# A transformer layer with routed experts on one core: residual sums and their statistics moved ahead of the routing in VectorE's step

## What is computed

```python
# attention: Q, K, V are products of the normed x with wq, wk, wv (64 x 256 each)
energy  = einsum('bnd,bne->bde', K, V)
context = einsum('bnd,bde->bne', Q, energy) * sqrt(3/64)
x = x + einsum('bnd,ed->bne', context, wo)

# experts, on xn = layernorm(x)
scores = sigmoid(xn @ Wr)                       # 8 scores per token
_, idx = top_k(scores + router_bias, 2)
w  = take_along_axis(scores, idx); w = w / (sum(w) + 1e-9)
cw = zeros((T, 8)).at[rows, idx].add(w)
hid = silu(xn @ Wg[e]) * (xn @ Wu[e])           # e = 0..3, 256 -> 128
routed = sum_e cw[:, e] * (hid @ Wd[e])
routed += (cw[:, 4] + cw[:, 6]) * xn + cw[:, 7] * relu(xn)
shared = causal depthwise convolution of xn with 4 taps + conv_b
x = x + routed + shared
```

## Time and profile before

| | |
|---|---|
| median of 3 runs | 970.82 us (967.7 to 972.82) |
| the profiled execution: time, span | 970.19 us, 968.4 us |
| PE matmul busy | 917.5 us, 95% of the span |
| PE weight loads busy | 808.8 us, 84% |
| VectorE busy | 814.6 us, 84% |
| GpSimd busy | 553.8 us, 57% |
| ScalarE busy | 506.0 us, 52% |
| mean granted clock of TensorE | 0.983 |
| chain that ended last, by engine | PE 55%, DVE 26%, ACT 6%, POOL 6%, issue 5% |

### The profile page before, as it was taken

How to read it: one execution, slowest core, us unless ns; L and a number is a source line. 1 busy time by engine, 2 the same in 40 slices (tenths; PEclk the granted TensorE clock), 3 DMA queues, 4 the chain that set the end, 5 groups by cost and what they waited for, 6 DMA issues and landing times.

```text
span 968.4 us, 16869 instructions
## 1 busy us (share of the span) xinstructions
PE 917.5 (95%) x5816; PEld 808.8 (84%) x5816; DVE 814.6 (84%) x2294; ACT 506.0 (52%) x1003; POOL 553.8 (57%) x491
## 2 busy tenths in 40 slices
PE   4779999999999999999999999999999999988887
PEld 4668989888898888998898988988898988777776
DVE  6667889999889988999888998899888987776685
ACT  3454655555465555556555654656565545534432
POOL 2135755556576555656655566666556655655653
PEclk9788999999999999999999999999999999999989
DMA  6311333222133332223333211333322122221111
GB/s 178 116 44 45 109 110 110 99 99 77 56 110 110 110 109 71 72 78 110 110 109 110 89 68 65 110 110 110 110 88 80 41 79 88 88 88 66 65 64 47
DMA packets 61014, 87.10 MB, mean 90 GB/s; under 512 B 4480, under 2 KB 56832, under 8 KB 56832
## 3 DMA queue, kind: packets, MB, share of 16 engines
q1 hardware_dynamic: 60928, 86.01, 25.9%
HBM read 68.96 MB, written 17.04 MB: 89 GB/s over the span
## 4 chain that ended last, share of the span: by engine, by line
PE 55%; DVE 26%; ACT 6%; POOL 6%; issue 5%; DMA 1%; POOLq 0%; ACTq 0%; DVEq 0%
PE ps_gu L359 7%; PE ps_gu L361 7%; PE ps_gu L360 7%; PE ps_sh L464 5%; PE ps_y L359 4%; PE ps_y L360 4%; PE ps_y L361 4%; ACT x L676 4%; DVE stats L820 3%; POOL rstd L1012 3%; DVE acc L812 3%; PE ps_sh L454 2%; DVE chosen L863 2%; PE ps_y L407 2%; DVE hid L774 2%
## 5 line engine op out<-in xcount | busy, mean ns | idle before, releaser
L1030 POOL TENSOR_TENSOR gate<-gate,cwb 128x512 f32<-128x512 f32 x128 | 174.4, 1363 | 191.4 <-ACT gate L617 115.6
L359 PE MATMUL ps_gu<-x2T_hi,wgu_hi 128*128 128x512 f32 x512 | 212.7, 415 | 0.8 <-DVE hid L774 0.8
L360 PE MATMUL ps_gu<-x2T_lo,wgu_hi 128*128 128x512 f32 x512 | 203.3, 397 | 0.0
L361 PE MATMUL ps_gu<-x2T_hi,wgu_lo 128*128 128x512 f32 x512 | 203.1, 397 | 0.0
L1047 POOL TENSOR_TENSOR enx<-inv_e,logits 128x32 f32<-128x32 f32 x32 | 177.1, 5533 | 7.2 <-ACT logits L610 7.0
L617 ACT ACTIVATE gate<-ps_gu 128x512 f32<-128x512 f32 x128 | 76.0, 594 | 160.6 <-PE ps_gu L361 160.6
L359 PE MATMUL ps_y<-wd_hi,hid_hi 128*128 128x256 f32 x512 | 153.0, 299 | 4.0 <-POOL hid_lo L1035 3.5
L361 PE MATMUL ps_y<-wd_hi,hid_lo 128*128 128x256 f32 x512 | 145.1, 283 | 0.0
L360 PE MATMUL ps_y<-wd_lo,hid_hi 128*128 128x256 f32 x512 | 145.1, 283 | 0.0
L791 DVE SCALAR_TENSOR_TENSOR conv<-x2T,conv_w,conv 128x512 f32<-128x512 f32 x192 | 141.0, 773 | 0.0
L1009 POOL TENSOR_TENSOR mv<-mv,eps_ln 128x4 f32<-128x4 f32 x64 | 12.8, 199 | 184.1 <-DVE mv L823 156.5
(11 more groups left out here) (94 smaller groups left out, 1961.0 us busy)
## 6 DMA issues: line engine op xcount, KB each, us to landing
cwb<-cw_rows SPq DMA_DIRECT2D x32, 1024.0 KB, 4.7
xa<-in_x SPq DMA_DIRECT2D x32, 512.0 KB, 6.9
acc<-in_x SPq DMA_DIRECT2D x32, 512.0 KB, 5.9
out<-acc SPq DMA_DIRECT2D x64, 256.0 KB, 2.3
cwb<-in_wg SPq DMA_DIRECT2D x4, 128.0 KB, 2.7
cwb<-in_wu SPq DMA_DIRECT2D x4, 128.0 KB, 2.6
cwb<-in_wd SPq DMA_DIRECT2D x1, 512.0 KB, 4.1
cw_rows<-cwT SPq DMA_DIRECT2D x32, 8.0 KB, 1.3
```

The source lines that it names most:

```text
L359: nc.tensor.matmul(dst, a_hi, b_hi, start=start, stop=False, skip_group_check=True)
L360: nc.tensor.matmul(dst, a_hi, b_lo, start=False, stop=False, skip_group_check=True)
L361: return nc.tensor.matmul(dst, a_lo, b_hi, start=False, stop=stop, skip_group_check=True)
L1030: g.tensor_tensor(gate[:, e % 2], gate[:, e % 2], cwb[:, q, e], ALU.mult).then_inc(gatew_ready, 1)
```

## The change

Only VectorE's order inside a step changes; no instruction is added or removed. The first residual sum now stands in front of the third expert's product, the second one and the statistics directly behind it, and the routing after them. The third expert's low half follows the routing, then the fourth expert's product, then the relu term. Steps in which the routing works and the experts don't keep their order.

```diff
--- before.py
+++ after.py
@@ -954,24 +954,23 @@
                     dve.wait_ge(mhi_out, st.chains(1, 1))
                     v.tensor_tensor(m_lo[:, :, :], ps_gram[:, :].rearrange("p (c n) -> p c n", c=HC),
                                     m_hi[:, :, :].bitcast(F32), ALU.subtract).then_inc(mlo_out, 1)
+                if b_on:
+                    residual(st, 0)
+                if c_on:
+                    hidden(st, 2)
+                if b_on:
+                    residual(st, 1)
+                    norm2_stats(st)
+                if r_on:
+                    route(st)
+                if c_on:
+                    hid_low(st, 2)
+                    hidden(st, 3)
                 if c_on:
 
                     dve.wait_ge(relu_ready, st.before("C", TG, TG))
                     k = st.slot("C", 4)
                     v.tensor_tensor(acc[:, k], acc[:, k], x2[:, st.slot("C", 2)], ALU.add).then_inc(relu_added, 1)
-                    hidden(st, 2)
-                if r_on and c_on:
-                    route(st)
-                if c_on:
-                    hid_low(st, 2)
-                if b_on:
-                    residual(st, 0)
-                    residual(st, 1)
-                    norm2_stats(st)
-                if r_on and not c_on:
-                    route(st)
-                if c_on:
-                    hidden(st, 3)
                 if st.on("A"):
                     for c in range(HC):
                         q = st.slot("A", 4)
```

## The result

The changed kernel took 990.56 us (median of 4 executions, 983.2 to 993.5), the kernel before 970.04 us beside it: a ratio of 1.0196, 95% interval 1.0149 to 1.0243. In a later comparison it took 991.2 against 971.4 us, 1.018 (1.0142 to 1.0218). A ratio here is estimated with its interval and is not the quotient of the two medians beside it, which can lie some 0.4% off (here it is 1.021). The profiled execution is the quickest of its four, 983.2 us with a span of 981.4.

A forecast was written before the change was run, and what follows sets the result against it. TensorE was taken to bound most of the run. Late routing +21.1, the L454 wait -5.8 and the tail -1.8 gave +13.5 on 970.19, 983.7 us, stated as 984.0 for a median; 8-in-10 range 972 to 991.

The forecast's parts named there:

- TensorE is the bound, and two waits decide: At full load TensorE runs matmuls 112.07 of 112.43 us; VectorE's order matters only through what TensorE waits for.
- The wait before L454 goes: At x2_transpose 0, 100 to 829 us: earlier statistics remove TensorE's wait for the normed tiles x2, -5.8 us.
- The routing comes late by the hold: GpSimd's gate_weight 3 holds den 0.75 us; TensorE loses 0.81 us up to expert 2's down product, 26 steps: +21.1 us.
- No further cost behind the down product: After expert 2's down product, hidden 3 and the relu term end before ScalarE can begin x2; cover 0.7 us.
- The tail: From 827 us, without the Gram matrix: three steps 0.91 us shorter each, the first 0.9 longer, sum -1.8 us.
- The last two steps: The last two steps, without attention, gain or lose a few tenths of a microsecond.
- The sum: Whole kernel: +21.1 - 5.8 - 1.8 = +13.5 us on the profiled 970.19, giving 983.7; 984.0 us for a median.
- No hold: At den beside gate_weight 3: den and what follows get through while GpSimd works; 961 us, chance 0.08.
- part of the hold: In the routing: den slips through, the next two-tensor instruction is held only 0.3 us; 970 us, chance 0.13.
- more hold: gate_weight 3 slips and holds routing up to 1.3 us, or the relu term is held; 989 to 994 us, chance 0.10.
- rival 4: The same as more hold: 0.2 to 0.4 us more in a step, 989 to 994 us, chance 0.10.
- Slack on TensorE: TensorE's weight loads leave 12.89 of 112.43 us free, absorbing the wait for routing; 962.6 us, chance 0.04.

The follow-up runs named there:

- The first experiment: The changed kernel with one more wait on GpSimd, so gate_weight 3 starts only after the routing's third instruction: 966.1 us, ratio 0.9904 to the kernel before.

## Why the prediction was right, point by point

- **TensorE is the bound, and two waits decide.** Right. VectorE and GpSimd lost 35 and 24 us of busy time and nothing was gained by it.
- **The wait before L454 goes (-5.8).** Right; none is left. ScalarE's order was what came next.
- **The routing comes late by the hold (+0.81 a step, +21.1).** Right in each figure: den 0.89 us (reckoned from zero + 2.72 to + 3.61, 0.89), L499 at zero + 7.33 (7.33), the down product at zero + 8.13 (8.12). The first experiment takes the hold away and with it the loss. Four steps grew by 2.25 us; 4 x 0.81 less three waits of 0.34 before L454 is 2.2. Over the whole body, 25 steps, the profiles differ by 14.7 us; the 21.1 less 5.8 of the prediction, for 26 steps, are 15.3.
- **No further cost behind the down product.** Right for the new order. The relu term's cover held: it ends at 558.54 and x2 starts at 559.53. For the old order I carried the same reasoning over and was wrong, since I had looked at who waits for the relu term and not at whom it holds.
- **The tail (-1.8).** Right as a count of work, wrong as a forecast of time, because the clock is missing from it. TensorE is through x2_transpose 0 at zero + 12.8 wherever the clock is full (12.86 reckoned), and the four tail steps of the kernel with 12 idle products take 112.9 us against 114.9 before, -2.0. In the changed kernel itself they take 115.5 us in the first profile and 119.4 in the second: +0.7 and +4.5.
- **The last two steps (a few tenths).** This term was mis-sized. From the end of these four steps to the end of the span the kernel before takes 49.85 us and the changed one 46.6 in both profiles, -3.2. The granted clock there is 0.91 to 0.92 in the kernel before and 1.00 in the changed one. How much of the 3.2 us the clock makes was not separated.
- **The sum (983.7).** It met the profiled execution (983.2) partly by luck: the +0.7 instead of -1.8 in the tail steps and the -3.2 at the end cancel. A slip of 0.3 us stands in the last line too: 13.5 over the median of 970.82 is 984.3, not 984.0. The median is 990.6, 6.6 us above the forecast and 0.4 us inside the range, whose upper end had been drawn for more hold and not for the clock; that it lies inside is luck. The sum was put against one execution and took over its granted clock, while the kernel before runs at 0.982 in the median and the changed one at 0.973 to 0.974.
- **The rivals.** No hold, part of the hold and more hold are refuted by den's 0.89 us in the median of 32 and by the transposes at zero + 7.33. By the time alone the measured 990.6 us would have been rival 4's (989 to 994). Slack on TensorE by its weight loads is refuted as well: with weight loads running for 99.88 of 111.70 us the fastest of these steps had no idle time between matmuls, and each wait of the changed kernel appeared in the step's length. The Trainium skill (Trainium Kernel Development and Optimization, section Best Practices) would have seen room there; these rows show none.

## What to carry to other kernels

Before moving a chain of small VectorE instructions, lay GpSimd's instructions beside the new place as well as the old: an instruction of 0.14 us became one of 0.89 because a 1.29 us product began 0.44 us before it, and moving that product by one semaphore was worth 1.3% in the kernel before, while the reordering cost 2%. Ask of a moved instruction both what holds it and what it holds. And reckon idle time of TensorE twice, once as time and once as clock: filling waits of 2.9 us in the tail brought back some 6 to 7 us of granted clock. A sum made against one profile carries that profile's clock with it, on both sides of the comparison.

## What the runs showed of the hardware

- VectorE and GpSimd hold each other in both directions. den, chosen and raw (128x32 elements in SBUF), and wsum_eps (128x4, up to 0.96 us), when they start inside a GpSimd product, end 0.03 to 0.06 us behind it. The relu term, begun 0.07 us earlier, stretched GpSimd's power from 1.01 to 2.00 us. Batch norm aggregates (four in 0.36 us), maxima (four in 0.35 us) and sums with one operand in PSUM (0.67 to 0.69 us) passed beside the same product at their usual length. The Trainium skill (GPSIMD Engine Reference, section Key points) names the contention, with VectorE instructions that read two SBUF inputs or run in a 2-port mode. The rows of the two-input instructions agree and show its size here: the whole rest of the other's product. GpSimd's power is different: in the changed kernel one runs from 539.74 for 5.43 us, and VectorE's hid_lo, with two inputs, starts inside it at 541.34 and takes its usual 0.68. Whether den, which reads one tile, runs in such a mode no row shows.
- Twelve useless products in each tail step raised the granted clock there from 0.89 to 0.94 up to 1.00, and the kernel took 983.9 us in the median instead of 990.6 and 991.2. Twenty of them kept the clock up too and gained nothing (989.9 us). Twenty fp32 products of the 128x128 identity with itself are 40 records on TensorE, 0.11 us apart.
